# Softmax sums and attention values from one pass of 64-row matmul tiles, with the steps of all engines reordered

## The reference

```python
xn = layernorm(x); q = rope(xn @ Wq); k = rope(ctx @ Wk); v = ctx @ Wv
p = softmax(q @ k.T / 4)              # per sequence and head, 64 x 64
x = x + (p @ v) @ Wo
xn = layernorm(x); s = (xn @ Wq_w.T) @ keys.T     # 64 expert scores
gate = softmax of the top 16 of s, 0 elsewhere
x = x + ((xn @ A_w.T) * gate repeated 8 times) @ B_w.T * 2
```

## Time and profile before

| | before |
|---|---|
| median of 3 runs | 189.95 us (189.06 to 191.23) |
| the profiled execution: its own time | 191.24 us |
| the profiled execution: span of the trace | 189.5 us |
| PE busy | 177.6 us (94%) |
| DVE busy | 133.4 us (70%) |
| ACT busy | 89.3 us (47%) |
| POOL busy | 86.2 us (45%) |
| mean granted TensorE clock | 0.991 of full speed |

### The profile page before, as it was taken

How to read it: one execution, slowest core, us unless ns; L and a number is a source line. 1 busy time by engine, 2 the same in 40 slices (tenths; PEclk the granted TensorE clock), 3 DMA queues, 4 the chain that set the end, 5 groups by cost and what they waited for, 6 DMA issues and landing times.

```text
span 189.5 us, 3948 instructions
## 1 busy us (share of the span) xinstructions
PE 177.6 (94%) x1382; PEld 133.5 (70%) x1382; DVE 133.4 (70%) x375; ACT 89.3 (47%) x206; POOL 86.2 (45%) x112
## 2 busy tenths in 40 slices
PE   7999899988989999999999999999999995998884
PEld 2656483765878868886988788886878662587764
DVE  2678958797999586975697478838793776725661
ACT  3759779637263616454455626371525335303210
POOL 5589979758964504470427225340425023020300
PEclk9999999999999999999999999999999998799999
DMA  6999602010010301000020100010001000000111
GB/s 190 313 393 404 260 4 57 3 55 0 0 59 0 100 14 55 2 35 24 0 61 0 55 3 0 0 61 0 0 3 55 0 3 0 2 0 5 55 44 67
DMA packets 5331, 11.30 MB, mean 60 GB/s; under 512 B 688, under 2 KB 944, under 8 KB 5056
## 3 DMA queue, kind: packets, MB, share of 16 engines
q1 hardware_dynamic: 5024, 10.79, 16.4%
q10 hardware_dynamic: 288, 0.27, 0.4%
HBM read 8.95 MB, written 2.10 MB: 58 GB/s over the span
## 4 chain that ended last, share of the span: by engine, by line
PE 81%; DVE 8%; POOL 4%; issue 3%; ACT 2%; ACTq 0%; DVEq 0%; POOLq 0%
PE ps_w L996 12%; PE ps_w L997 11%; PE ps_w L1001 11%; PE ps_t L1009 7%; PE ps_s L1056 6%; PE ps_w L1153 4%; PE ps_s L1088 4%; PE ps_s L1094 4%; PE ps_s L1075 3%; PE ps_t L1014 3%; PE ps_w L1145 3%; PE ps_w L989 3%; DVE neg_top L731 3%; POOL b_lo L248 2%; PE ps_w L990 2%
## 5 line engine op out<-in xcount | busy, mean ns | idle before, releaser
L305 POOL TENSOR_TENSOR late<-late,gate 128x512 f32<-128x512 f32 x7 | 7.6, 1082 | 42.9 <-issue 27.8
L731 DVE TENSOR_REDUCE neg_top<-ps_s 128x8 f32<-128x512 f32 x32 | 20.0, 682 | 2.0 <-PE ps_s L1056 2.0
L483 ACT ACTIVATE eT<-ps_s 128x512 f32<-128x512 f32 x32 | 16.5, 605 | 4.3 <-PE ps_s L1081 4.2
L271 POOL TENSOR_TENSOR q_r<-q_a,q_b 128x512 f32<-128x512 f32 x7 | 9.1, 1295 | 17.3 <-DVE q_b L716 17.3
L996 PE MATMUL ps_w<-am_hi,x2T_hi 128*128 128x288 f32 x52 | 15.0, 310 | 1.6 <-ACT x2T_hi L504 1.6
L290 POOL TENSOR_TENSOR oT_lo<-o_n,oT_hi 128x512 fp32r<-128x512 f32 x8 | 10.2, 1276 | 12.5 <-ACT oT_hi L491 12.5
L996 PE MATMUL ps_w<-b_hi,zT_hi 128*128 128x512 f32 (+1 forms) x32 | 12.7, 401 | 1.9 <-ACT zT_hi L531 1.9
L997 PE MATMUL ps_w<-am_lo,x2T_hi 128*128 128x288 f32 x52 | 14.2, 296 | 0.0
L476 ACT ACTIVATE mT<-ps_t 128x256 fp32r<-128x256 f32 x8 | 3.1, 384 | 21.5 <-PE ps_t L1065 21.5
L996 PE MATMUL ps_w<-wo_hi,oT_hi 128*128 128x512 f32 x32 | 12.8, 401 | 0.0
L997 PE MATMUL ps_w<-wo_lo,oT_hi 128*128 128x512 f32 x32 | 12.6, 395 | 0.0
(11 more groups left out here) (192 smaller groups left out, 535.1 us busy)
## 6 DMA issues: line engine op xcount, KB each, us to landing
x_sb<-x SPq DMA_DIRECT2D x8, 256.0 KB, 7.4
cT_in<-cT SPq DMA_DIRECT2D x7, 256.0 KB, 3.2
out<-res SPq DMA_DIRECT2D x7, 256.0 KB, 2.0
wq_sb<-wq SPq DMA_DIRECT2D x4, 256.0 KB, 6.9
late<-wo SPq DMA_DIRECT2D x1, 1024.0 KB, 9.3
am_sb<-aT SPq DMA_DIRECT2D x1, 1024.0 KB, 8.3
b_sb<-bT SPq DMA_DIRECT2D x1, 1024.0 KB, 7.0
wkv_sb<-wkv SPq DMA_DIRECT2D x1, 512.0 KB, 4.6
```

Source lines behind the costliest of these rows:

```text
L271: pool.tensor_tensor(q_r[:].rearrange("p (r k d) -> p k r d", r=REP, k=KVH), q_a[:].rearrange("p (k r d) -> p k r d", r=REP, k=KVH), q_b[: ...
L483: act.activation(eT[:, c].rearrange("p b n -> p (b n)"), ps_s[:, c, :], ACT.Exp)\
L731: dve.tensor_reduce(neg_top[:, :, b, HALF_H * half:HALF_H * (half + 1)], ps_s[:, 2 * (1 - b) + half, :].rearrange("p (r h k) -> p r h k", ...
```

## The change

`values(t)` loses the matmuls with `pair_ones`. The memory of `v_bd` is filled with ones instead of zeros, and V is written over its block diagonal: the 64 rows of head h hold V in 16 of the 32 columns and ones in the other 16. One group of sixteen matmuls over 64 rows each (b, c, h) then gives values and sums, head h in PSUM bank h. `attend(t)` turns both banks (1,024 columns) in one instruction, takes the reciprocals, multiplies in the turned layout and turns the product back; in steps 2 to 5 `q_low(n)` is issued between its first and second instruction. `scores(t, 1)` waits for that first instruction only, no longer for `o_n`. The orders of all engines and the choice between `ps_t0` and `ps_t1` change too. `x_low(p)` moves from the end of a step to the start of the next; `k_blocks` works a tile further ahead; two of the four `b_lo` splits move from step 1 to `second()`. `values_out` now comes before `rotate_k` for tiles 3 on: ACT reads the bank first, and DVE waits for it.

```diff
-        ps_o, ps_sum = ps_s[:, 0, :], ps_s[:, 1, :]
+        ps_o = ps_s[:, 0:2, :]
...
-            pool.memset(v_bd[:], 0.0).then_inc(v_zero, 1)
+            pool.memset(v_bd[:], 1.0).then_inc(v_ones, 1)
...
                 o_low(0)
                 split_lo(am_lo, am_sb, am_hi, am_h, am_l, 2)
                 split_lo(am_lo, am_sb, am_hi, am_h, am_l, 3)
+                split_lo(b_lo, b_sb, b_hi, b_h, b_l, 0)
                 rotated_q(2)
                 c_low(3)
+                split_lo(b_lo, b_sb, b_hi, b_h, b_l, 1)
             def step(i):
                 f, n, p = i - 1, i + 1, i + 2
                 if p + 1 < T:
                     deviation1(p + 1)
                 deviation2(f)
-                k_blocks(n, 0)
-                k_blocks(n, 1)
                 if i == 1:
-                    for k in range(DK):
-                        split_lo(b_lo, b_sb, b_hi, b_h, b_l, k)
+                    k_blocks(n, 0)
+                    k_blocks(n, 1)
                 gated(f)
+                if i == 1:
+                    split_lo(b_lo, b_sb, b_hi, b_h, b_l, 2)
+                    split_lo(b_lo, b_sb, b_hi, b_h, b_l, 3)
                 o_low(i)
+                k_blocks(p, 0)
+                k_blocks(p, 1)
                 if p + 1 < T:
                     c_low(p + 1)
                 rotated_q(p)
...
             def step(i):
                 f, n, p = i - 1, i + 1, i + 2
                 x2_high(f)
-                for c in range(PAIRS):
+                for c in range(PAIRS - 1):
                     exps(i, c)
                 expert_scores(f)
+                exps(i, PAIRS - 1)
                 z_first(f)
                 expert_exps(f)
+                q_high(n)
                 z_second(f)
-                q_high(n)
+                values_out(p)
                 o_high(i)
+                k_high(p)
                 z_high(f)
-                values_out(p)
                 if p + 1 < T:
                     normalise(p + 1)
                     c_high(p + 1)
                 value_blocks(p)
                 m_out(n)
+                x2_centre(i)
                 if p + 1 < T:
                     x_high(p + 1)
-                x2_centre(i)
-                k_high(p)
...
                 dve.wait_ge(kv_ps, t + 1)
+                if t >= RAW:
+                    dve.wait_ge(v_st_ok, t + 1)
...
-            def attend(t):
-                dve.wait_ge(sum_ps, t + 1)
-                dve.transpose(sum_t[:], ps_sum).then_inc(inv_step, 1)
-                dve.wait_ge(inv_step, 3 * t + 1)
-                dve.reciprocal(inv_c[:], sum_t[:].rearrange("p (u h d) -> p u h d", h=2, d=HD)[:, :, :, 0])\
-                   .then_inc(inv_step, 1)
-                dve.wait_ge(inv_step, 3 * t + 2)
-                dve.transpose(inv[:], inv_c[:].unsqueeze(3).broadcast_to([P, HD, 2, HD])).then_inc(inv_step, 1)
-                dve.wait_ge(inv_step, 3 * t + 3)
+            def attend(t, meanwhile=lambda: None):
+                n = 3 * t
                 dve.wait_ge(o_ps, t + 1)
+                dve.transpose(o_s[:].rearrange("p h u g d -> p (h u g d)"),
+                              ps_o.rearrange("p h n -> p (h n)")).then_inc(o_step, 1)
+                meanwhile()
+                dve.wait_ge(o_step, n + 1)
+                for h in range(2):
+                    mm = dve.reciprocal(inv[:, h, :], o_s[:, h, :, 1 - h, 0])
+                mm.then_inc(o_step, 1)
+                dve.wait_ge(o_step, n + 2)
+                for h in range(2):
+                    mm = dve.tensor_tensor(o_t[:, :, h, :], o_s[:, h, :, h, :],
+                                           inv[:, h, :].unsqueeze(2).broadcast_to([P, HD, HD]), ALU.mult)
+                mm.then_inc(o_step, 1)
+                dve.wait_ge(o_step, n + 3)
                 if t >= 1:
                     dve.wait_ge(oT_lo_ok, t)
-                dve.tensor_tensor(o_n[:], ps_o, inv[:], ALU.mult).then_inc(o_ok, 1)
+                dve.transpose(o_n[:], o_t[:].rearrange("p u g d -> p (u g d)")).then_inc(o_ok, 1)
...
             def step(i):
                 f, n, p = i - 1, i + 1, i + 2
                 x2_low(f)
+                if p > RAW:
+                    x_low(p)
                 if p + 2 < T:
                     statistics1(p + 2)
                 route(f)
-                attend(i)
-                q_low(n)
+                if i == 1:
+                    q_low(n)
+                    attend(i)
+                else:
+                    attend(i, lambda: q_low(n))
                 rotate_k(p)
-                z_low(f)
                 top(n, 0)
                 top(n, 1)
+                k_low(p)
+                rotate_q(p)
                 m_parts(n)
-                rotate_q(p)
+                z_low(f)
                 residual(i)
-                if p + 1 < T:
-                    x_low(p + 1)
                 statistics2(i)
-                k_low(p)
...
                     else:
-                        pe.wait_ge(o_ok, t)
+                        pe.wait_ge(o_step, 3 * t - 2)
...
             def values(t):
                 pe.wait_ge(exp_ok, 4 * t + 4)
-                for c in range(PAIRS):
-                    mm = pe.matmul(ps_sum[QUAD * c:QUAD * (c + 1), :], pair_ones[:],
-                                   eT[:, c].rearrange("p b n -> p (b n)"), start=True, stop=True)
-                mm.then_inc(sum_ps, 1)
                 pe.wait_ge(v_bd_ok, 4 * t + 4)
                 for b in range(2):
                     for c in range(PAIRS):
-                        mm = pe.matmul(ps_o[QUAD * c:QUAD * (c + 1), 2 * P * b:2 * P * (b + 1)],
-                                       v_bd[:, t % 2, b, c, :], eT[:, c, b, :], start=True, stop=True)
+                        for h in range(2):
+                            rows = slice(ROWS * h, ROWS * (h + 1))
+                            mm = pe.matmul(ps_o[QUAD * c:QUAD * (c + 1), h, 2 * P * b:2 * P * (b + 1)],
+                                           v_bd[rows, t % 2, b, c, :], eT[rows, c, b, :], start=True, stop=True)
                 mm.then_inc(o_ps, 1)
...
-                    pe.wait_ge(x_lo_ok, i)
+                    pe.wait_ge(mT_ok, i + 1)
                     turn_x2(f)
                     turned_scores(i)
+                pe.wait_ge(x2_ok, i)
+                project_down(f, 0)
+                if i >= 2:
                     pe.wait_ge(res_ok, f)
                     project_q(p, [0])
-                pe.wait_ge(x2_ok, i)
-                project_down(f, 0)
                 project_q(p, [1])
                 values(i)
                 pe.wait_ge(x2T_lo_ok, i)
...
                 project_q(p, [2])
                 pe.wait_ge(z_ok, 2 * i)
                 project_kv(p)
+                scores(n, 0)
+                scores(n, 1)
                 pe.wait_ge(kT_lo_ok, n + 1)
                 turn_zg(f)
-                scores(n, 0)
-                scores(n, 1)
                 project_q(p, [3]).then_inc(q_ps, 1)
+                pe.wait_ge(qT_lo_ok, n + 1)
+                turn_k(p)
                 pe.wait_ge(v_st_ok, p + 1)
                 project_out(i)
-                pe.wait_ge(zT_lo_ok, i)
-                turn_m(n)
-                if p + 1 < T:
-                    pe.wait_ge(qT_lo_ok, n + 1)
-                    turn_xh(p + 1, ps_t0)
                 pe.wait_ge(q_rot, 2 * p + 2)
                 up_high(f)
+                pe.wait_ge(kT_lo_ok, p + 1)
+                turn_m(n)
                 up_low(f)
-                pe.wait_ge(mT_ok, n + 1)
-                turn_k(p)
+                if p + 1 < T:
+                    turn_xh(p + 1)
-                pe.wait_ge(qT_lo_ok, m + 1)
+                pe.wait_ge(mT_ok, m + 1)
                 turn_x2(a)
                 turned_scores(m)
                 pe.wait_ge(x2_ok, m)
```

More of the change, by code:

```diff
@@ L122, in build @@
         router_sb = eT[0:ROUTER].rearrange("p c b n -> p (c b n)")[:, 0:D + E]
-        sum_t, inv_c, inv = sb("sum_t", [P, D]), sb("inv_c", [P, HD, 2]), sb("inv", [P, D])
-        o_n = sb("o_n", [P, D])
+        o_s, inv = sb("o_s", [P, 2, HD, 2, HD]), sb("inv", [P, 2, HD])
+        o_t, o_n = sb("o_t", [P, HD, 2, HD]), sb("o_n", [P, D])
         oT_hi = sb("oT_hi", [P, REP, 2, BATCH], F32R)
@@ L155, in x2_of, with xhT_bank, kT_bank, mT_bank @@
             return x2[:, t % 2, :] if t < T - 1 else xh[:]
+        def xhT_bank(t):
+            return ps_t1 if t == 1 or t > RAW else ps_t0
+        def kT_bank(t):
+            return (ps_t1 if t < RAW else ps_t0)[:, 0:P]
+        def mT_bank(t):
+            return (ps_t1 if t < 2 or t == T - 1 else ps_t0)[:, 0:2 * P]
         def up_bank(half):
@@ L165, in build @@
         warm_ok, ident_ok, mask_ok, pick_ok = sem("warm_ok"), sem("ident_ok"), sem("mask_ok"), sem("pick_ok")
-        ones_ok, sel_ok, const_ok, mask_step = sem("ones_ok"), sem("sel_ok"), sem("const_ok"), sem("mask_step")
-        v_zero = sem("v_zero")
+        sel_ok, const_ok, mask_step = sem("sel_ok"), sem("const_ok"), sem("mask_step")
```

(37 more changed lines are left out.)

14 lines of the change are left out of this document (6 added, 8 removed).

## The result

The kernel after the change takes **194.67 us** (median of 4 runs, 194.08 to 194.92) against 190.59 (189.06 to 191.29) for the kernel before on the same chip: ratio 1.021, 95% interval 1.016 to 1.027. It is slower; whether by more than 2% the interval leaves open. The forecast was 185.2 with a range up to 190.9; what happened is the rival that had a chance of 0.12.

A forecast was written before the change was run, and what follows sets the result against it. PE was taken to bound the kernel, busy 177.6 of 189.5 us. Savings of 3.4 (steps 2 to 5), 0.8 (ramp, step 1) and 0.5 us (`last()`), 4.7 together, took the median 189.95 to 185.2 us; range 182.0 to 190.9.

The forecast's parts named there:

- the rival that had a chance of 0.12: Middle steps: POOL's `o_low` starts before `k_r`, then `m_parts` is late too; step 21.2 us, whole 193.8; chance 0.12.
- The pass, 0.86 us per tile: Matmuls of `values` on PE: row halves overlap, so sums and values take 1.00 us instead of 1.86.
- DVE, +0.7 per tile: `attend` on DVE: the new instructions sum to 3.2 us against 2.5 before, +0.7 us per tile.
- A middle step, -0.86: Steps 2 to 5: new waits bind nowhere, a step falls from 20.32 to 19.46 us; -3.4 us over these steps.
- The walk: Predicted times of each engine's instructions through a middle step, counted from the start of `turn_x2`, giving 19.46 us.
- `m_parts` blocked twice: Middle steps: POOL's `c_low` and `rotated_q` delay both `m_parts` instructions; step 20.6 us, whole 191.0; chance 0.08.
- Ramp and step 1, -0.8: Ramp and step 1: `values(1)` and fewer `b_lo` splits save more than DVE's delays cost; -0.8 us.
- `last()`, -0.5: Tail: half the pass saved at a low clock in `values(l)`, less delays; -0.5 us, range +0.5 to -1.5.

The follow-up runs named there:

- e9: The changed kernel with `rotate_k` reading the bank of k and v ahead of `values_out` again, for tiles 3 on: 188.56 us.
- e3: The changed kernel with POOL in steps 1 to 5 waiting for `k_r` before `o_low`: 188.57 us.
- e4: The changed kernel with POOL in steps 1 to 5 waiting for `m_parts` before `c_low`: 190.25 us.
- e5: The changed kernel with both holds on POOL, `o_low` waiting for `k_r` and `c_low` for `m_parts`: 187.65 us.
- e10: e5 with the two `b_lo` splits of step 1 placed behind `o_low`: 186.80 us.
- e2: The changed kernel with the old `values` and `attend` put back, so the new orders alone: 198.17 us.

## Why the prediction was wrong

- **The pass, 0.86 us per tile: right.** 1.02 us against 1.86, 0.84; the row halves overlap.
- **DVE, +0.7 per tile: right as work.** From 112.67 to 116.31 less 0.58 for `q_low` is 3.06 us against 2.5, so +0.6. The large turn took 1.24, as set.
- **A middle step, -0.86: the step that failed.** In the prediction's words, `values_out` ahead of `rotate_k` was "hidden", "since DVE is in `attend` until then". DVE was done with `attend` at 116.31, and `k_a` waited until 117.33 for `v_st`; without the new wait (e9) it starts right behind `project_kv`, some 0.4 us sooner. The walk had `k_r` done at "about 11.5", so started at about 11.2, and ahead of `o_low` by "less than 0.3"; it started at 117.86 - 106.55 = 11.31, and `o_low` at 11.28. So the walk was good to 0.2 us here, but the outcome hung on less than 0.3, and the forecast took the favourable side with 0.48 against 0.12. With `k_r` free (e3, e9) the step is 19.59 and 19.58, forecast 19.46: the sum was right, the order of `k_r` and `o_low` was not.
- **The rival that came true: right in its cause, its price in part by luck.** It had 21.2 us for a step against 21.36, and 193.8 for the whole against 194.67. But it counted on a `k_r` alone that ends 0.8 to 1.2 us late, which costs a step 0.62 (e4 against e5); the 1.77 need the blocked `m_parts` as well. It charged four steps 0.9 each, where steps 2 to 4 lost 1.04 and step 5 lost 0.1. The ramp and step 1 together lost 1.53 where it had 0.8, and the tail hid 1.46.
- **What followed from it:** `q_b` and `m_parts` late. Counted from `turn_x2`, `project_out` starts at 13.15 in the changed kernel and in e3 alike, `up_high` at 16.54 against 16.03, `turn_m` at 19.20 against 17.90. Of the 1.75 us between the two in step 4, 0.51 come from `q_b`, 0.79 from `m_split`, and 0.45 behind it, 0.37 of them where `up_low` waits for `z_low`, which stands behind `m_parts` on DVE.
- **`m_parts` blocked twice, as its own case (20.6):** not tested as it was priced. In e3 its two instructions took 1.89 us instead of 0.50, but, counted from `turn_x2`, they started at 15.31 and were done at 17.24, not at 18.3, and the step was 19.59. The waits that the case named, of `turn_m` and `up_low`, came in the changed kernel, where `m_parts` started at 16.41.
- **Ramp and step 1, -0.8: wrong sign.** Step 2 starts at 63.82 instead of 62.29, +1.53: +0.84 in the ramp and +0.69 in step 1. The forecast had seen the collision with `am_lo` and charged 0.5. It had not looked at `attend(1)`, whose products met the `b_lo` splits now behind `gated` (2.03 us), nor at `c_low` against `m_parts` in step 1. e5 takes 1.14 of this back, e10 another 0.9.
- **`last()`, -0.5: right in sign by luck.** The tail took 44.60 instead of 46.06, -1.46. But the forecast expected the low clock at `values(l)` again, since the idle time before it stays; it stayed (2.17 us), and the clock did not fall. e2, with the old pass and no fall of the clock, has a tail of 44.5, so nothing here shows a gain of the pass in the tail. The two kinds of executions of the kernel before differ by 2.1 us; if that is this fall of the clock, its tail would be about 44.0 without it (an estimate: 46.06 - 2.1), and the change then made the tail some 0.6 longer, and the whole loss is about 5 us rather than 3.3.
- **The chances:** 0.70 for faster rested on a walk whose margin at the decisive place was about the size of its error. A tie of 0.3 us that is worth 1.8 us in each of the middle steps (21.36 against 19.58) is a coin to be tossed, and the slower case should have had about 0.4.

One more thing beside the tie. The Trainium skill, GPSIMD Engine Reference, section Specifications, says that GpSimd contends with DVE instructions that have two SBUF inputs or run in a 2-port performance mode. The runs here block the two-input ones (`k_r`, the products, the second of `m_parts`), and the copy of `m_parts` too, which has one input: 0.21 us in e4, 1.32 in the changed kernel. Whether that is the second half of the rule no run here shows; the prediction put the copy and `k_r` under the rule on two inputs, and for the copy that reason does not hold.
